# Two chained feed-forward stages: another order of their steps on ScalarE and TensorE, and an earlier first slot for all stages from the second one on

## The chip, the cores and the metric

The kernel runs on one core of a Trainium2 chip. Its time is device microseconds for one launch, taken as the median of the runs shown. Engine names are those of the profile: PE is TensorE's matmul side and PEld its weight loads, DVE is VectorE, ACT is ScalarE, POOL is GpSimd, SP is SyncE, which here only issues DMAs.

## What is computed

The input x has 128 sequences of 64 rows of 128 numbers. Four layers follow one another, and each adds two terms to x: a cross-attention of some kind and a feed-forward of some kind, each applied to the layer-normalised x and weighed by the tanh of a gate. The two feed-forwards that this change touches are those of layers 0 and 1. Both multiply with a 128x128 weight in 8-bit arithmetic:

```python
# layer 0 (lhs is layernorm(x))
lhs_scale = max(abs(lhs), over a row) / 127
acc = round(lhs / lhs_scale) @ round(rhs / rhs_scale)
x = x + gate * acc * lhs_scale * rhs_scale
# layer 1 (x is layernorm(x))
a_scale = max(abs(x), over a row)
y = round(x / a_scale * 127) @ w_quant.T
x = x + gate * y * (w_scale * a_scale / 127)
```

Between them stands layer 1's masked softmax attention (16 heads of 8), and behind them come layer 2's retention, layer 2's gated feed-forward, layer 3's softmax attention and, last and longest, layer 3's switch attention with routed experts.

## The kernel before, in words

x stays in SBUF as 64 tiles of 128 rows. After an opening (weights, context, layer 0's attention), the function `chain` runs six parts one behind the other and overlapping: `ff0` (feed-forward of layer 0), `at1` (softmax attention of layer 1), `ff1` (feed-forward of layer 1), `re` (retention), `gf` (gated feed-forward), `at3` (softmax attention of layer 3). Then `switch_attention` runs, which fills a little under two thirds of the span.

A part is a list of steps for each engine, each with a lag. Time is counted in slots. A part that begins at slot S and has pace 1 gives its item i to a step of lag L in slot S + i + L; with pace 2 it takes two items in a slot. `chained` writes out, for each engine, all steps of all parts in order of slot, within a slot in the order of the parts, and within a part in the order of the step list. So each engine's queue is a fixed order, and semaphores alone hold the engines together: a step that waits holds up everything behind it on its engine. The slots are no clock; an engine can be about a slot ahead of another.

`feed_forward_int` builds ff0 and ff1. Its item is a group of 4 tiles (16 groups). With the lag of each step in brackets, a group g goes through: DVE row statistics, aggregation and variance (1), POOL reciprocal root `rstd` (1), DVE negated mean (3), ACT `normalise` (3), DVE `absmax`, `scale`, `inverse` and, in layer 1, the output scale (4), ACT `shift` (5), which multiplies by 127 over the largest value and adds a large constant so that the sum is rounded, PE `turned` (5), four transposes into PSUM, ACT `keep` (6), which copies them to SBUF as bf16 and takes the constant off, PE `product` (6), DVE `output` (7), POOL `add` (7). In layer 0 POOL also spreads rows of layer 0's attention (`spread`, 0), PE turns them (0), DVE adds them to x (1), and POOL weighs the output before it adds it (7). In the order before, ACT's list is keep, normalise, shift, and PE's is product, turned.

`softmax_attention` (at1) has one tile per slot and begins at slot 12. Its lags run from 0 (row statistics) to 14 (the last addition to x, L1058), with normalise at 6 and the negated mean at 5, the projections at 8, the scores at 9, their reading, centring and exponential at 10, the turning of the probabilities at 11, the weighing of the values at 12. Tile 63 is therefore read last in slot 12 + 63 + 14 = 89. ff1's `turned` and `product` write PSUM banks in which at1 keeps its scores, and wait for at1's last score to be read (`after["turned"]`, slot 85). `re` waits for at1's last tile before it writes its SBUF buffers. In every slot that ff1 shares with at1, at1's steps stand ahead of ff1's on each engine; in a slot that ff0 shares with at1, ff0's stand ahead.

Of the kernel before, what the change touches and what calls it, by code (L numbers as in the profile page):

```python
# [54 lines left out]
def chained(parts, engine, eng):  # L55

    stages = [part.engines[engine](eng) if engine in part.engines else [] for part in parts]
    slots = [(part.start + t / part.pace, n, t) for n, part in enumerate(parts) if stages[n]
             for t in range(part.count + max(lag for lag, _ in stages[n]))]
    for _, n, t in sorted(slots):  # L60
        for lag, step in stages[n]:
            i = t - lag
            if 0 <= i < parts[n].count:
                step(i, i % parts[n].bufs, i // parts[n].bufs)


def once(step):

    def at(i, s, r):
        if i == 0:  # L70
            step()
    return at
# [685 lines left out]
def feed_forward_int(k, A, C, W, X, layer, OUT0, after):  # L758
# [113 lines left out]
    def scalar(act):  # L872
        def begin():
            act.preload_act_table(ACT.Exp)

        def normalise(g, s, r):
            act.wait_ge(q["nmr"], g + 1)
            for n in range(N):
                act.activation(xhat[:, s, n], tile(g, n), ACT.Identity, bias=small["nmr"][:, s, n:n + 1],
                               scale=small["rstd"][:, s, n:n + 1]).then_inc(q["xhat"], 1)  # L880

        def keep(g, s, r):
            act.wait_ge(q["turned"], g + 1)
            if g >= NB:
                act.wait_ge(q["product"], g - NB + 1)
            act.activation(qT[:, s], ps_q[g % 2], ACT.Copy, bias=-ROUND).then_inc(q["qT"], 1)

        def shift(g, s, r):
            act.wait_ge(q["inverse"], g + 1)
            if g >= NB:  # L890
                act.wait_ge(q["turned"], g - NB + 1)
            for n in range(N):
                act.activation(shifted[:, s, n], xhat[:, s, n], ACT.Copy, bias=ROUND,
                               scale=small["inv"][:, s, n:n + 1]).then_inc(q["shifted"], 1)
        return [(0, once(begin)), (6, keep), (3, normalise), (5, shift)]

    def tensor(pe):
        def turn_rows(g, s, r):
            pe.wait_ge(q["spread"], 2 * g + 2)
            if g >= 2:  # L900
                pe.wait_ge(q["added"], g - 1)
            for n in range(N):
                m = pe.transpose(ps_rows[g % 2][:, n], rows[:, g % 2, n], C["ident"][:])
            m.then_inc(q["rows"], 1)

        def turned(g, s, r):
            pe.wait_ge(q["shifted"], N * g + N)
            if g == 0 and layer == 1:
                pe.wait_ge(*after["turned"])
            if g >= 2:  # L910
                pe.wait_ge(q["qT"], g - 1)
            for n in range(N):
                m = pe.transpose(ps_q[g % 2][:, n], shifted[:, s, n], C["ident"][:])
            m.then_inc(q["turned"], 1)

        def product(g, s, r):
            pe.wait_ge(q["qT"], g + 1)
            if g == 0 and layer == 1:
                pe.wait_ge(*after["product"])
            if g >= 2:  # L920
                pe.wait_ge(q["y"], g - 1)
            for n in range(N):
                m = pe.matmul(ps_y[g % 2][:, n], qT[:, s, n], w16[:], start=True, stop=True)
            m.then_inc(q["product"], 1)
        return ([(0, turn_rows)] if layer == 0 else []) + [(6, product), (5, turned)]
    return Part(q, GROUPS, NB, gpsimd=gpsimd, vector=vector, scalar=scalar, tensor=tensor)


# [1428 lines left out]
def chain(k, A, C, W, X, CT, OUT0, x3):  # L2357

    nc = k.nc
    waits = {n: {} for n in ("at1", "ff1", "re", "gf", "at3")}
    with k.laid_over():
        at1 = softmax_attention(k, A, C, W, X, CT, 1, waits["at1"])
    with k.laid_over():
        at3 = softmax_attention(k, A, C, W, X, CT, 3, waits["at3"], x3)
    with k.laid_over(sbuf=False):
        re = retention(k, A, C, X, waits["re"])
    with k.laid_over():
        ff0 = feed_forward_int(k, A, C, W, X, 0, OUT0, {})  # L2370
    with k.laid_over():
        ff1 = feed_forward_int(k, A, C, W, X, 1, None, waits["ff1"])
    with k.laid_over(sbuf=False):
        gf = feed_forward_gated(k, A, C, W, X, waits["gf"])
    G, T = GROUPS, TILES
    waits["at1"].update(x=lambda i: (ff0.q["x"], i // GROUP + 1), a=(ff0.q["added"], G), qkv=(ff0.q["added"], G),
                        scores=(ff0.q["y"], G))
    waits["ff1"].update(buffers=(ff0.q["x"], G), x=at1.q["x"], turned=(at1.q["masked"], T), product=(at1.q["masked"], T))
    waits["re"].update(buffers=(at1.q["x"], T), x=ff1.q["x"], s1=(ff1.q["qT"], G), o=(ff1.q["y"], G))
    waits["gf"].update(buffers=(ff1.q["x"], G), x=re.q["x"], turn_x=(re.q["kT"], G), down=(re.q["x"], T),  # L2380
                       gate_up={0: [(re.q["wide"], HEADS // 2 * G), (re.q["probs"], T - 1)], 1: [(re.q["probs"], T)]},
                       turn_h={0: [(re.q["probs"], T)], 1: [(re.q["x"], T - 1)]})
    waits["at3"].update(buffers=(re.q["x"], T), x=lambda i: (gf.q["x"], i + 1), a=(gf.q["xT"], G),
                        qkv=(gf.q["hidden"], T), turned=(gf.q["hidden"], T), scores=(gf.q["hT"], T), o=(gf.q["x"], T))
    parts = [ff0.begins(0, 1), at1.begins(12, 1), ff1.begins(83, 1), re.begins(97, 2), gf.begins(131, 2), at3.begins(166, 2)]
    with nc.Block() as block:
        @block.sync
        def _(sp):
            chained(parts, "sync", sp)

        @block.gpsimd
        def _(pool):
            chained(parts, "gpsimd", pool)

        @block.vector
        def _(dve):
            chained(parts, "vector", dve)

        @block.scalar
        def _(act):  # L2400
            chained(parts, "scalar", act)

        @block.tensor
        def _(pe):
            chained(parts, "tensor", pe)
# [3 lines left out]
def program(nc, A, out):  # L2409
    k = Core(nc)  # L2410
    C, W = {}, {}
    scratch = {n: nc.dram_tensor("scratch_" + n, [S * 4 * S * 2], F32, kind="Internal") for n in ("lags", "circ")}
    x3 = nc.dram_tensor("scratch_x", [TILES * P * D], F32, kind="Internal").ap()\
        .rearrange("(t p d) -> t p d", p=P, d=D)
    with k.stack:
        constants(k, C)
        with k.scope():
            X = k.sb("x", [P, TILES, D])
            CT = k.sb("ctx_T", [P, TILES, P])
            prepared_weights(k, W)  # L2420
            OUT0 = k.sb("out0", [P, 2, TILES, 4])
            opening(k, A, C, W, X, CT, OUT0, scratch)
            with k.scope():
                chain(k, A, C, W, X, CT, OUT0, x3)
        switch_attention(k, A, C, x3, out)
# [23 lines left out]
```

## Time and profile before

| what | value |
|---|---|
| runs (median of 3) | 3125.66 us (3125.22, 3125.66, 3128.91) |
| the profiled execution's own time | 3124.05 us |
| its span, first to last instruction | 3122.3 us |
| granted TensorE clock over the span | 0.938 of full speed |
| PE, PEld busy | 92%, 70% |
| DVE, ACT, POOL busy | 87%, 75%, 70% |
| first step of ff0 / last addition of ff1 to x | 79.6 us / 546.5 us |

The profiled execution is 1.75 us longer than its span, and 1.6 us shorter than the median. The clock column of the profile is the share of full speed that was granted to TensorE; of its two levels 1.00 is 2.4 GHz and 0.50 is 1.2 GHz.

### The profile page before, as it was taken

To read this page: it belongs to the slowest core of one execution; us is meant where nothing else is said; L and a number is where in the kernel's file an instruction comes from. 1 tells how busy PE (TensorE), PEld (TensorE's weight loads), DVE (VectorE), ACT (ScalarE), POOL (GpSimd) and SP (SyncE) were. 2 spreads that over 40 slices of the span, in tenths; PEclk is the share of its full clock that TensorE was granted. 3 is DMA by queue.
4 is the path that set the end of the run, shared out by engine and by line. 5 is a ranking of instruction groups with operands and counts; after the bars stand their busy time and mean duration, and the time that the engine had idled before them with its cause. 6 is when DMAs were issued, how large, how long until landed. Compare 5 with 4: busy or idle time off the path is not lost.

```text
span 3122.3 us, 80587 instructions
## 1 busy us (share of the span) xinstructions
PE 2878.7 (92%) x25631; PEld 2189.3 (70%) x25644; DVE 2724.0 (87%) x9025; ACT 2348.9 (75%) x7674; POOL 2180.3 (70%) x3016
## 2 busy tenths in 40 slices
PE   7599984996689996999999999999999999999998
PEld 6367762674367774777777777777777777777776
DVE  6779977999979987988988889889889888898897
ACT  5667777779968875777777777777777777777776
POOL 2788866657944424777777777777777777777777
PEclk8589995997779997999999999999999999999999
DMA  5000001220000004000000000000000000000000
GB/s 132 8 2 3 3 2 31 76 68 1 1 8 18 18 20 130 7 9 7 9 8 7 9 8 7 9 8 7 9 7 9 8 7 9 8 7 9 8 6 6
DMA packets 114661, 55.46 MB, mean 18 GB/s; under 512 B 18496, under 2 KB 113856, under 8 KB 114240
## 3 DMA queue, kind: packets, MB, share of 16 engines
q1 hardware_dynamic: 114240, 50.30, 5.9%
q8 instruction: 209, 3.42, 0.5%
q14 instruction: 212, 1.74, 0.2%
HBM read 41.82 MB, written 8.45 MB: 16 GB/s over the span
## 4 chain that ended last, share of the span: by engine, by line
PE 60%; DVE 1%; ACT 1%; POOL 0%; issue 0%; DMA 0%; SPq 0%; POOLq 0%; ACTq 0%; DVEq 0%
PE ps_sw_a L2283 24%; PE ps_sw_d L2283 22%; PE ps_sw_w L2329 4%; PE ps_sw_w L2316 3%; PE ps_sw_s L2298 2%; PE ps_sw_s L2340 2%; PE ps_sw_m L2305 1%; ACT sw_scaled L2024 0%; DVE sw_v_part L2179 0%; PE ps_sw_m L2291 0%; DMA sw_v<-in_L_ffn_v_w 0%; ACT sw_probs L2073 0%; DVE sw_o_low L2125 0%; DVE sw_v_low L2118 0%; ACT sw_v_high L2079 0%
## 5 line engine op out<-in xcount | busy, mean ns | idle before, releaser
L2024 ACT ACTIVATE sw_scaled<-ps_sw_a,sw_gate_o 128x128 f32<-128x128 f32 x2048 | 620.4, 447 | 253.9 <-PE ps_sw_a L2283 246.7
L2024 ACT ACTIVATE sw_scaled<-ps_sw_a,sw_gate_v 128x128 f32<-128x128 f32 x2048 | 597.7, 449 | 193.8 <-PE ps_sw_a L2283 192.1
L2179 DVE SCALAR_TENSOR_TENSOR sw_o_part<-ps_sw_d,sw_gate_o,sw_o_part 128x128 f32<-128x128 f32 x1920 | 555.4, 339 | 62.8 <-PE ps_sw_d L2283 60.2
L1951 POOL TENSOR_TENSOR sw_v_pair<-sw_v_part,sw_scaled 128x256 f32<-128x256 f32 x512 | 382.1, 746 | 154.6 <-DVE sw_v_part L2179 88.5
L2179 DVE SCALAR_TENSOR_TENSOR sw_v_part<-ps_sw_d,sw_gate_v,sw_scaled 128x128 f32<-128x128 f32 x1024 | 304.2, 338 | 123.5 <-PE ps_sw_d L2283 106.4
L1977 POOL TENSOR_TENSOR sw_o_rest<-sw_o_rest,sw_scaled 128x256 f32<-128x256 f32 x384 | 285.3, 743 | 157.7 <-ACT sw_scaled L2024 120.5
L2179 DVE SCALAR_TENSOR_TENSOR sw_v_part<-ps_sw_d,sw_gate_v,sw_v_part 128x128 f32<-128x128 f32 x1024 | 305.1, 339 | 0.0
L1980 POOL TENSOR_TENSOR sw_o_rest<-sw_o_rest,sw_scaled 128x256 f32<-128x256 f32 x384 | 282.9, 737 | 30.1
L1956 POOL TENSOR_TENSOR sw_v<-sw_v_pair 128x128 f32<-128x128 f32 x512 | 244.2, 477 | 40.1
L2283 PE MATMUL ps_sw_a<-sw_v_high,sw_xT_high 128*128 128x512 f32 x512 | 234.1, 457 | 8.2 <-DVE sw_v_low L2118 8.2
L2283 PE MATMUL ps_sw_a<-sw_o_high,sw_ctx_high 128*128 128x512 f32 x512 | 215.5, 421 | 0.2 <-ACT sw_scaled L2024 0.2
L1030 POOL TENSOR_TENSOR at_key_wide<-at_keyT,c_quarter_heads 128x512 f32<-128x512 f32 x128 | 133.1, 1040 | 109.5 <-ACT at_keyT L1168 109.5
L2283 PE MATMUL ps_sw_d<-sw_v_high,sw_xT_high 128*128 128x512 f32 x512 | 207.5, 405 | 0.4 <-DVE sw_v_part L2179 0.4
L2283 PE MATMUL ps_sw_d<-sw_o_high,sw_ctx_high 128*128 128x512 f32 x512 | 202.1, 395 | 1.2 <-DVE sw_v_part L2179 1.2
L2283 PE MATMUL ps_sw_d<-sw_o_low,sw_ctx_high 128*128 128x512 f32 x512 | 202.8, 396 | 0.0
L2283 PE MATMUL ps_sw_a<-sw_o_high,sw_ctx_low 128*128 128x512 f32 x512 | 202.7, 396 | 0.0
L2283 PE MATMUL ps_sw_a<-sw_v_high,sw_xT_low 128*128 128x512 f32 x512 | 202.0, 395 | 0.0
L2283 PE MATMUL ps_sw_d<-sw_o_high,sw_ctx_low 128*128 128x512 f32 x512 | 202.0, 395 | 0.0
L2283 PE MATMUL ps_sw_a<-sw_o_low,sw_ctx_high 128*128 128x512 f32 x512 | 201.9, 394 | 0.0
L2283 PE MATMUL ps_sw_d<-sw_v_high,sw_xT_low 128*128 128x512 f32 x512 | 201.5, 394 | 0.0
L2283 PE MATMUL ps_sw_a<-sw_v_low,sw_xT_high 128*128 128x512 f32 x512 | 201.5, 394 | 0.0
L2283 PE MATMUL ps_sw_d<-sw_v_low,sw_xT_high 128*128 128x512 f32 x512 | 200.2, 391 | 0.0
(337 smaller groups left out, 8467.2 us busy)
## 6 DMA issues: line engine op xcount, KB each, us to landing
re_values<-in_ctx SPq DMA_DIRECT2D x128, 64.0 KB, 2.3
l_ctx<-in_ctx SPq DMA_DIRECT2D x16, 256.0 KB, 5.4
x<-in_x SPq DMA_DIRECT2D x16, 256.0 KB, 5.4
re_ctx<-in_ctx SPq DMA_DIRECT2D x16, 256.0 KB, 3.1
scratch_x<-x SPq DMA_DIRECT2D x64, 64.0 KB, 1.5
sw_x<-scratch_x SPq DMA_DIRECT2D x64, 64.0 KB, 1.9
sw_x_res<-scratch_x SPq DMA_DIRECT2D x64, 64.0 KB, 1.8
out<-sw_y SPq DMA_DIRECT2D x64, 64.0 KB, 1.5
```

The costliest lines, as they stand in the source:

```text
L1030: pool.tensor_tensor(key_wide[:, s], keyT[:, s].unsqueeze(1).broadcast_to([P, QUARTER, P]), C["quarter_heads"][:].unsqueeze(2).broadcast_t ...
L1951: pool.tensor_tensor(v_pair[:, h % 2], v_part[:, h], scaled[:, h % 4, 2:4], ALU.add)\
L1956: pool.tensor_tensor(v[:, h], v_pair[:, h % 2, 0], v_pair[:, h % 2, 1], ALU.add).then_inc(q["v"], 1)
L1977: pool.tensor_tensor(o_rest[:, 0:2], o_rest[:, 0:2], scaled[:, h % 4, 0:2], ALU.add)\
L1980: pool.tensor_tensor(o_rest[:, 2:4], o_rest[:, 2:4], scaled[:, h % 4, 2:4], ALU.add)\
L2024: act.activation(scaled[:, h % 4, e], ps_a[h % 2][:, e], ACT.Copy, scale=gates[:, s, h, HALF_E + e:HALF_E + e + 1]).then_inc(a_scaled[kind ...
L2179: dve.scalar_tensor_tensor(out=acc[:, e % 2], in0=ps_d[h % 2][:, e], scalar=gates[:, s, h, e:e + 1], in1=before, op0=ALU.mult, op1=ALU.add ...
L2283: m = pe.matmul(bank, lhs[a], w[b][:, h, experts], start=c == 0, stop=c == 2)
L2298: m = pe.matmul(ps_s[t, h], probs[t, s, h], C["ident"][t, t], start=True, stop=True)
L2316: m = pe.matmul(ps_w[n][:, h * P:(h + 1) * P], W["pair"][:, 4 * n + h], xT[:, s], start=True, stop=True)
L2329: m = pe.matmul(ps_w[b][:, h * S:(h + 1) * S], v[t, h], probs_T[t, h], start=True, stop=True)
L2340: m = pe.matmul(ps_s[t], xT[:, s, t], uT[:, :, t], start=True, stop=True)
```

## The change

The step lists of `feed_forward_int` are reordered on two engines, for both feed-forwards, and four start slots in `chain` are lowered by three. No instruction is added or removed, none changes its shape, and no wait is changed.

```diff
-        return [(0, once(begin)), (6, keep), (3, normalise), (5, shift)]
+        return [(0, once(begin)), (3, normalise), (5, shift), (6, keep)]
...
-        return ([(0, turn_rows)] if layer == 0 else []) + [(6, product), (5, turned)]
+        return ([(0, turn_rows)] if layer == 0 else []) + [(5, turned), (6, product)]
...
-    parts = [ff0.begins(0, 1), at1.begins(12, 1), ff1.begins(83, 1), re.begins(97, 2), gf.begins(131, 2), at3.begins(166, 2)]
+    parts = [ff0.begins(0, 1), at1.begins(12, 1), ff1.begins(80, 1), re.begins(94, 2), gf.begins(128, 2), at3.begins(163, 2)]
```

The first line is ACT's list, the second PE's. ff1's groups now go through slots 81 to 102 in place of 84 to 105, retention and what follows keep their distance to ff1.

## Rows read from the trace of the kernel before

**Rows 1.** The page: span, and the granted clock in 40 slices
```profile
span 3122.3 us, 80587 instructions
...
PEclk8589995997779997999999999999999999999999
```

**Rows 2.** Windows: us, busy time of each engine (instructions), granted clock, DMA share, GB/s
```profile
96.00:141.00 45.00, 26.32 (x120) 19.26 (x120) 36.13 (x168) 32.95 (x91) 38.94 (x47) 0.50 0.00 1
...
190.00:440.00 250.00, 245.02 (x4090) 188.78 (x4090) 227.26 (x552) 196.99 (x453) 203.51 (x183) 1.00 0.01 3
433.45:454.00 20.55, 17.07 (x287) 12.70 (x283) 16.95 (x45) 13.83 (x27) 14.79 (x12) 0.99 0.01 2
454.00:472.03 18.03, 9.58 (x88) 7.91 (x88) 10.64 (x63) 11.62 (x31) 4.28 (x5) 0.50 0.10 30
472.03:503.16 31.13, 12.05 (x56) 7.41 (x56) 20.09 (x107) 22.74 (x63) 16.08 (x15) 0.50 0.06 18
```

**Rows 3.** Timeline of ACT in ff1: start, us, engine, line, operation [idle before <-releaser]
```profile
495.70 0.60 ACT L886 ACTIVATE ff_qT<-ps_ff_q 128x512 bf16<-128x512 f32 x1 [1.20 <-PE ps_ff_q L913]
496.19 1.63 ACT L879 ACTIVATE ff_xhat<-x,ff_nmr,ff_rstd 128x128 f32<-128x128 f32 x4
497.73 1.27 ACT L893 ACTIVATE ff_shifted<-ff_xhat,ff_inv 128x128 f32<-128x128 f32 x4
500.20 0.60 ACT L886 ACTIVATE ff_qT<-ps_ff_q 128x512 bf16<-128x512 f32 x1 [1.20 <-PE ps_ff_q L913]
```

**Rows 4.** Timeline of PE in that slot of ff1
```profile
499.05 1.11 PE L913 MATMUL ps_ff_q<-c_ident,ff_shifted 128*128 128x128 f32 x4 [2.09 <-ACT ff_shifted L893]
```

**Rows 5.** Timeline of DVE, the same slot of ff1
```profile
497.86 0.69 DVE L817 TENSOR_REDUCE ff_amax<-ff_xhat 128x4 f32<-128x512 f32 x1 [1.62 <-ACT ff_xhat L879]
...
500.50 0.17 DVE L866 TENSOR_SCALAR ff_var<-ff_mv 128x4 f32<-128x4 f32 x1
500.58 0.16 DVE L811 SCALAR_TENSOR_TENSOR ff_nmr<-ff_mv,ff_rstd 128x4 f32<-128x4 f32 x1
```

**Rows 6.** Timeline of POOL in ff0, one slot
```profile
118.26 0.73 POOL L801 COPY ff_rows<-out 128x256 f32<-128x256 f32 x2
119.22 1.02 POOL L786 TENSOR_TENSOR ff_rstd<-ff_var,minus_half 128x4 f32<-128x4 f32 x1 [0.22 <-DVE ff_var L866]
120.21 1.27 POOL L792 TENSOR_TENSOR ff_y<-ff_y,w_ff_scale 128x512 f32<-128x512 f32 x1
121.55 1.27 POOL L795 TENSOR_TENSOR x<-x,ff_y 128x512 f32<-128x512 f32 x1
```

**Rows 7.** Timeline where at1 begins beside ff0
```profile
152.88 0.48 ACT L1135 ACTIVATE at_xhat<-x,at_nmr,at_rstd 128x128 f32<-128x128 f32 x1
...
157.35 0.28 ACT L1174 ACTIVATE at_xT<-ps_at_a 128x128 f32<-128x128 f32 x1 [1.03 <-PE ps_at_a L1263]
```

**Rows 8.** Timeline of DVE and POOL: short DVE steps beside POOL's
```profile
510.46 1.02 POOL L786 TENSOR_TENSOR ff_rstd<-ff_var,minus_half 128x4 f32<-128x4 f32 x1 [2.97 <-DVE ff_var L866]
...
510.68 0.13 DVE L811 SCALAR_TENSOR_TENSOR ff_nmr<-ff_mv,ff_rstd 128x4 f32<-128x4 f32 x1
...
511.45 1.27 POOL L795 TENSOR_TENSOR x<-x,ff_y 128x512 f32<-128x512 f32 x1
512.08 0.67 DVE L828 TENSOR_SCALAR ff_scale<-ff_amax 128x4 f32<-128x4 f32 x1
...
550.77 1.71 DVE L1394 SCALAR_TENSOR_TENSOR re_nmr<-re_mv,re_rstd 128x4 f32<-128x4 f32 x1
550.84 1.62 POOL L1359 TENSOR_TENSOR re_k_part<-re_ctx,re_rot 128x256 f32<-128x256 f32 x2
```

**Rows 9.** Timeline of DVE where at1 ends beside ff1
```profile
433.45 0.28 DVE L1058 TENSOR_TENSOR x<-ps_at_a,x 128x128 f32<-128x128 f32 x1
...
472.03 0.86 DVE L839 BATCH_NORM_STATS2 ff_stats<-x 128x6 f32<-128x128 f32 x4
```

**Rows 10.** Source view of L1058: count, ns min/median/max, first and last start us
```profile
L1058 DVE TENSOR_TENSOR x<-ps_at_a,x x64: 280/281/292, 190.4 to 468.8; 128x128 f32<-128x128 f32 x64
```

## The prediction

> **What bounds the kernel now.** The page comes first: it gives the span, and its clock row shows two dips in the first 900 us, at the second to fourth slice and at the sixth and seventh [rows 1]. The windows over these stretches tell what goes on there. Between 190 and 440 us, where at1 runs alone, PE is busy 98% at full clock. Beside ff0 (96 to 141) and in ff1 (472 to 503) TensorE has half the clock and PE is busy 58% and 39% of the time, and no other engine is full either: in ff1 ACT has 22.7 us of 31.1, DVE 20.1, POOL 16.1 [rows 2]. Where nothing is full, a loop of waits sets the pace, and the timeline of one slot shows which.
>
> On ACT the keep starts at 495.70 behind 1.20 us of idle time that ended with PE's transposes; then normalise, then shift; the next keep starts at 500.20, again behind 1.20 us [rows 3]. PE's transposes start at 499.05, when the shift is done, and take 1.11 [rows 4]. So the slot of 4.50 us is keep 0.49, normalise 1.54, shift 1.27, transposes with their semaphores 1.20. The transposes of a group run behind its shift, and ACT has nothing to do in between, since keep stands at the head of its list. DVE waits 1.62 us for the normalised group in each slot: of 4.50 it works 2.88 [rows 5].
>
> **The reorder in ff1.** With keep at the end of the slot the transposes it needs were made in the slot before, during ACT's own work. What remains on ACT is 0.49 + 1.54 + about 1.2 = 3.25 us a slot. I check the others against that: DVE 2.88 of work [rows 5], POOL 1.02 for the root and 1.27 for the addition = 2.3 [rows 8], PE 1.11 and a product shorter than that. The product now waits for a keep that comes last, and DVE's output takes it in the next slot, some 4.0 us after the slot's normalise began; output, aggregation, variance and negated mean behind it need 1.2 more, and the normalise that they release is due at 6.5. So that loop has 1.3 us in hand. ACT sets 3.25.
>
> The slots that hold ff1 alone are 90 to 96 before: from the seventh group's statistics at 472.03 to 503.16, 31.1 us for 7 [rows 2, 9]. Three of them go away by the earlier start, and the other four take 4 x 3.25 = 13.0. Lower bound of the slot 2.9 (DVE's work), upper 4.5 (as before).
>
> **The earlier start.** It takes no work away: three slots' worth of ff1 moves from slots of its own into slots 81 to 83 of at1, and each later group meets more of at1 than it did. Before, slots 81 to 89 last from 433.45 to 472.03, 38.6 us [rows 9]. An at1 slot takes 4.4 us (the first to the 64th addition is 278.4 us for 63 slots [rows 10]), with DVE busy 91%, 4.0 us a slot, of which some 0.6 has run out by slot 81 (the row statistics of at1), so 3.4. To this come 1.4 of ff1's row steps in slots 81 to 83 and 2.3 in 84 and 85 (DVE's 2.88 less the output), while at1's own part falls to about 2.9. That is 4.8, 4.8, 4.9, 5.2, 5.3, DVE-bound, sum 25.0. In 86 to 89 the clock is at half, as before [rows 2], PE has at1's last turns and weighings together with ff1's transposes, and at1's steps of each slot start behind a product that waits for the late keep; I take 6.0, 4.7, 4.5, 3.8, sum 19.0 (from 454 to 472, about the same four slots, it was 18.0 [rows 2]). Waits that such a sum does not hold, and ff1's table load, which moves to slot 80 where ACT has less spare time: 2.7. Together 46.7, 8.1 more than before. Bounds: 41.6, if the added steps go into idle time as far as there is any, and 58, if each shared slot runs the chains of both parts one after the other.
>
> ff1 and at1's end: 38.6 + 31.1 before, 46.7 + 13.0 after, gain 10.0.
>
> **Beside retention.** In its slots 94 to 96 ff1 still has all its steps and retention adds mostly DVE work (memsets, statistics), so DVE binds at about 4.0 where the loop had 4.5: 1.5 us. From then on DVE was the bound before already, and I add 0.5 for the keeps that waited. Gain 2.0, bounds 0 and 4. All parts behind keep their distance to each other and their periods: nothing. SP's fetches for retention wait for at1's last tile and still have five slots of ff1 in front of their first reader.
>
> **The reorder in ff0.** The same loop gives 4.50 there, but POOL is nearly full: 38.9 of 45.0 [rows 2]. One slot goes from 118.26 to the next spread at 122.77, with 0.22 idle; spread, root, weighing and addition make 4.3 [rows 6]. So the nine slots 7 to 15 gain 0.2 each, 1.8. Slot 6, before POOL's additions start, gains 0.7. In slot 16 spread is over, but at1's first root joins root, weighing and addition: 4.5 again, no gain, and DVE stands until that root is there, since at1's first negated mean is in its list before ff0's next steps. In slots 17 and 18 POOL has only 2.3 to 3.5, and ACT's 3.25 against 4.50 counts: 1.2 each. So at1's first normalise (slot 18, behind ff0's three steps on ACT), now at 152.88 [rows 7], comes 0.7 + 1.8 + 2.4 = 4.9 us earlier. In slots 19 to 22 ff0 runs out; the keep no longer waits there either, but PE now has the product behind the transposes, and at1's first matmuls behind both. I take these as cancelling, less 0.3: 4.6. The bounds are 1.8 (only POOL's slots gain) and 7.5 (the 1.2 counts in slots 6 and 17 to 20, five times, beside the 1.8).
>
> **Sum.** 10.0 + 2.0 + 4.6 = 16.6. The profiled execution took 3124.05, so 3107.45, and the median of the runs is 1.6 above it: 3109.
>
> **The locks between DVE and POOL** could undo part of it. DVE's scale of 128x4 numbers, 0.17 us alone, took 0.67 when it was issued at 512.08 beside POOL's addition, and ended with it at 512.75; the negated mean at 510.68 took 0.13 beside POOL's root, so the root does not hold it [rows 8]. In the new slot of ff1 POOL has root and addition back to back behind DVE's variance, busy until 2.4 us after it. The scale is issued about 0.8 us after the variance, in the root, and is not held; if ACT makes DVE wait it falls into the addition and is held for up to 1.27, which the slot that DVE is ahead absorbs. So I count nothing. At 550.77, though, a short step took 1.71 us, across both of two POOL steps that followed each other [rows 8]; if that happened here, the scale would wait 1.6 us, and DVE's slot would be 2.88 + 1.6 = 4.5, no better than before. The Trainium skill (SBUF — State Buffer, "Who interferes with whom") says that the port pair the two engines share is an exclusive lock, held for a whole instruction, so that the second to issue blocks fully. The addition's row agrees (0.67 for 0.17), the root's row does not (0.13). By that rule alone the root would hold the scale too, 0.35 us a slot: 3.23, still within ACT's 3.25, unless the lock passes straight to the addition, which is the rival below.
>
> **Rivals.**
> Locks set ff1's slot (4.45 in place of 3.25) and keep ff0's nine slots at 4.50: 4 x 1.2 + 1.8 = 6.6 less, 3116. For it speaks the row of 1.71, against it that of 0.67 with POOL's next step free to start. Chance 0.12.
> The clock falls earlier. PE's share in slots 81 to 85 goes down as these get longer, and the clock went to half in this stretch already, at about 454 [rows 2]. At half, at1's 4.3 us of matmuls a slot (98% of 4.4) take up to twice as long, some 7 against my 4.8 to 5.3; for four slots about 8 us: 3117. Chance 0.15.
> The shared slots take nearly nothing, since DVE and ACT both had idle time: the lower bound 41.6 gives 5 more, and ff0's upper bound 3 more: 3101. Chance 0.12.
> Slower: both junctions go serial. PE's list puts the product, which waits for the last copy of a slot, ahead of all of at1's steps of the next, and these feed ACT. If the shared slots of ff1 reach the upper bound of 58, ff1's side becomes 58 + 13 = 71 against 69.7, and the same coupling takes ff0's 4.6 and some more: 3127 to 3132. It decides from about 57 us for slots 81 to 89, 6.3 a slot. Against it: the last four of them took 4.5 each before [rows 2]. Chance 0.03.
> Nothing changes, since the start was not what held ff1 and the order binds elsewhere: 3126, 0.03; the 1.20 of idle time in each slot speaks against it.
>
> **Numbers.** Forecast 0.55, by its own range 3104 to 3114. The range 3101 to 3119 takes in the locks, the clock and the cheap overlap. What a measurement of this kernel can tell from no change is about 0.2%, 6.3 us: faster than 3119.4 I give 0.9, within 0.2% 0.06, slower 0.04.
>
> **What would show it.** ff1's keep in slots 90 to 93 every 3.2 to 3.3 us with no idle time before it, the normalise not waiting; absmax's wait of 1.62 gone; ff0's keeps every 4.3 us with POOL without gaps; at1's last addition to x later behind its first by some 8 us than now. Wrong: ff_scale with a mean well over 0.17, a keep period over 4 in ff1, the clock at 0.5 before at1's scores are through, or at1's first normalise less than 3 us earlier.

## The result, and the profile of the changed kernel

The median over the runs is 3122.36 us (3117.05 to 3133.31, 22 runs) against 3128.83 us of the kernel before (3125.22 to 3135.24, 22 runs on the same chip). The ratio is 0.9980 with a 95% interval of 0.9972 to 0.9987: 6 us faster by ratio and medians, where 16.6 was forecast. (The forecast of 3109 was made from a median before of 3125.66; that median is 3128.83 here, so 3.2 us of the 13 between forecast and time are not the change's.) The profiled execution took 3119.42 us around a span of 3117.6, 4.7 us less than the span of before [rows 1].

The page of the changed kernel, its first line and its clock row. The two dips of the clock are still there.

```profile
span 3117.6 us, 80600 instructions
...
PEclk8589985997789997999999999999999999999999
```

Windows of the changed kernel. The columns are those of [rows 2]. Slot 81 begins at 429.91, at the 56th addition to x of at1 (433.45 before), slot 90 at 486.62, with ff1's statistics there (472.03 before), and slot 94, retention's first, at 499.14. Slot 94 of this kernel stands against slot 97 of the kernel before, at 503.16.

```profile
96.00:141.00 45.00, 26.02 (x128) 21.62 (x128) 42.35 (x179) 34.94 (x97) 40.02 (x48) 0.50 0.00 1
429.91:450.00 20.09, 14.89 (x248) 10.95 (x244) 19.71 (x64) 13.97 (x31) 14.22 (x12) 1.00 0.00 1
450.00:486.62 36.62, 16.37 (x144) 14.00 (x141) 19.86 (x90) 20.77 (x56) 10.12 (x9) 0.50 0.07 19
486.62:499.10 12.48, 5.89 (x33) 4.58 (x32) 11.43 (x61) 12.48 (x37) 8.99 (x9) 0.50 0.11 33
```

This table is the finding: **slots 81 to 89 took 56.7 us in place of 38.6**, the slots of ff1 alone 12.5 (four) in place of 31.1 (seven). Of the 18.6 us won behind slot 90, 18.1 were paid ahead of it. DVE is full until 450 (19.71 of 20.09, where a slot takes 5.6 against 4.5 before); from 450 to 486.62 no engine is: ACT has 20.77 of 36.62, DVE 19.86, PE 16.37. That is again the picture of a loop of waits, the one that the reorder took out of ff1's own slots, now in the slots that ff1 shares with at1.

In ff1's own slots ACT works without a break. Its timeline there answers to [rows 3]: the keep no longer waits, and the period is 3.18 us, against 4.50.

```profile
489.07 0.57 ACT L886 ACTIVATE ff_qT<-ps_ff_q 128x512 bf16<-128x512 f32 x1
489.55 1.64 ACT L879 ACTIVATE ff_xhat<-x,ff_nmr,ff_rstd 128x128 f32<-128x128 f32 x4
491.08 1.27 ACT L893 ACTIVATE ff_shifted<-ff_xhat,ff_inv 128x128 f32<-128x128 f32 x4
492.25 0.58 ACT L886 ACTIVATE ff_qT<-ps_ff_q 128x512 bf16<-128x512 f32 x1
```

DVE in the same slot, against [rows 5]: the reduction follows the negated mean at once, and the 1.62 us of waiting ahead of it are gone.

```profile
488.70 0.16 DVE L811 SCALAR_TENSOR_TENSOR ff_nmr<-ff_mv,ff_rstd 128x4 f32<-128x4 f32 x1
488.78 0.68 DVE L817 TENSOR_REDUCE ff_amax<-ff_xhat 128x4 f32<-128x512 f32 x1
```

Now the shared slots, first one row of slot 81 and POOL's beside it. DVE's variance step, 0.17 us elsewhere, takes 0.88 and ends at 433.03, with POOL's step at 433.01:

```profile
431.97 1.04 POOL L1030 TENSOR_TENSOR at_key_wide<-at_keyT,c_quarter_heads 128x512 f32<-128x512 f32 x1
...
432.15 0.88 DVE L866 TENSOR_SCALAR ff_var<-ff_mv 128x4 f32<-128x4 f32 x1
```

Then slot 85 and parts of 86, all engines, rows picked out in order of time. Read what stands in brackets first: it is the idle time of the engine ahead of the row, and what ended it.

```profile
452.35 0.28 DVE L1058 TENSOR_TENSOR x<-ps_at_a,x 128x128 f32<-128x128 f32 x1
...
452.51 1.90 POOL L1023 TENSOR_TENSOR at_probs<-at_raw,at_top 128x1024 f32<-128x1024 f32 x1 [1.41 <-DVE at_top L1086]
...
452.83 0.29 DVE L1066 TENSOR_TENSOR at_heads_out<-ps_at_o,at_rsum 128x128 f32<-128x128 f32 x1
453.04 1.39 DVE L811 SCALAR_TENSOR_TENSOR ff_nmr<-ff_mv,ff_rstd 128x4 f32<-128x4 f32 x1
...
454.45 1.06 ACT L1159 ACTIVATE at_probs<-at_probs 128x1024 f32<-128x1024 f32 x1 [1.44 <-POOL at_probs L1023]
...
455.41 1.63 ACT L879 ACTIVATE ff_xhat<-x,ff_nmr,ff_rstd 128x128 f32<-128x128 f32 x4
...
456.95 1.26 ACT L893 ACTIVATE ff_shifted<-ff_xhat,ff_inv 128x128 f32<-128x128 f32 x4
...
458.27 1.12 PE L913 MATMUL ps_ff_q<-c_ident,ff_shifted 128*128 128x128 f32 x4 [5.89 <-ACT ff_shifted L893]
...
459.18 0.42 PE L1194 MATMUL ps_at_a<-c_ident,at_heads_out 128*128 128x128 f32 x1
...
460.11 0.28 ACT L1144 ACTIVATE at_heads_T<-ps_at_a 128x128 f32<-128x128 f32 x1 [1.90 <-PE ps_at_a L1194]
460.48 0.29 DVE L1058 TENSOR_TENSOR x<-ps_at_a,x 128x128 f32<-128x128 f32 x1 [3.92 <-ACT at_heads_T L1144]
...
466.99 0.58 ACT L886 ACTIVATE ff_qT<-ps_ff_q 128x512 bf16<-128x512 f32 x1
...
468.05 0.63 PE L923 MATMUL ps_ff_y<-w_ff,ff_qT 128*128 128x128 bf16 x4
...
469.78 0.29 DVE L1058 TENSOR_TENSOR x<-ps_at_a,x 128x128 f32<-128x128 f32 x1 [4.25 <-ACT at_heads_T L1144]
```

Slot 85 lasts from 452.35 to 460.48, 8.1 us (an at1 slot alone takes 4.4). The chain through it: at1's centre on POOL (1.9), the exponential on ACT behind it, then ff1's normalise and shift, which stand behind the exponential in ACT's list. PE stands still for 5.89 us for that shift, since ff1's transposes (L913) are next in its list. Behind them in the same list is at1's turn of the heads of slot 86 (L1194), whose input DVE had made by 453.12 (L1066). It runs at 459.18, ACT copies its result at 460.11, and DVE, after 3.92 us of idle time, adds to x at 460.48. In slot 86 the product (L923), behind the keep of 466.99, comes ahead of the next turn of the heads in the same way, and DVE idles 4.25 us. Two of the rows show a second, smaller loss: DVE's negated mean, 0.15 us elsewhere, takes 1.39 at 453.04 and ends with POOL's centre. The same step took 1.07 in slot 83 and 1.40 in slot 84. In slots 81 to 84, where DVE is full, the time by which its short steps are held comes to 3.0 us (0.71 and 0.14 for the variance in 81 and 82, 0.92 and 1.25 for the negated mean in 83 and 84).

In ff0, POOL's timeline of one slot, to be held against [rows 6]: root, next spread and next root follow without idle time, and from root to root it takes 4.39 us.

```profile
113.84 1.02 POOL L786 TENSOR_TENSOR ff_rstd<-ff_var,minus_half 128x4 f32<-128x4 f32 x1
...
117.38 0.74 POOL L801 COPY ff_rows<-out 128x256 f32<-128x256 f32 x2
118.23 1.02 POOL L786 TENSOR_TENSOR ff_rstd<-ff_var,minus_half 128x4 f32<-128x4 f32 x1
```

The first normalise of at1, which stood at 152.88 [rows 7]:

```profile
149.19 0.48 ACT L1135 ACTIVATE at_xhat<-x,at_nmr,at_rstd 128x128 f32<-128x128 f32 x1
```

Counted from ff0's first statistics (82.31 before, 82.44 here) that is 66.75 us against 70.57, 3.8 less.

### The profile page after: what moved, and what is told of

Same layout as the page of the kernel before. It is cut to its first block, busy times and chain, and to the rows that moved or that the text cites. A ratio compares the mean times of both kernels' runs of the same rounds, so it can differ in the third digit from the quotient of the medians.

```text
span 3117.6 us, 80600 instructions
## 1 busy us (share of the span) xinstructions
PE 2875.1 (92%) x25644; PEld 2192.7 (70%) x25644; DVE 2735.1 (88%) x9025; ACT 2352.2 (75%) x7674; POOL 2185.0 (70%) x3016
## 4 chain that ended last, share of the span: by engine, by line
PE 60%; ACT 1%; DVE 1%; POOL 0%; issue 0%; DMA 0%; SPq 0%; POOLq 0%; ACTq 0%
PE ps_sw_a L2283 24%; PE ps_sw_d L2283 22%; PE ps_sw_w L2329 4%; PE ps_sw_w L2316 3%; PE ps_sw_s L2298 2%; PE ps_sw_s L2340 2%; PE ps_sw_m L2305 1%; ACT sw_scaled L2024 0%; PE ps_sw_m L2291 0%; DVE sw_v_part L2179 0%; DVE sw_v_low L2118 0%; ACT sw_probs L2073 0%; DMA sw_v<-in_L_ffn_v_w 0%; ACT sw_v_high L2079 0%; PE ps_sw_w L2346 0%
## 5 line engine op out<-in xcount | busy, mean ns | idle before, releaser
L2073 ACT ACTIVATE sw_probs<-ps_sw_s,sw_shift 128x64 f32<-128x64 f32 x512 | 197.4, 479 | 4.6 <-DVE sw_shift L2240 4.6
```

What stands on the lines that cost most here:

```text
L2073: act.activation(probs[:, s, h], ps_s[:, h], ACT.Exp, bias=shift[:, s, h:h + 1], scale=float(P) ** -0.5, accum_out=total[:, s, h:h + 1]).t ...
```

## The experiments

The table gives all runs at a glance, and the text behind it takes them by the question that each answers. "Shared" is from the start of slot 81 to that of slot 90, "alone" from there to retention's first slot, read from the profiled run as above. The sum of the two is the time from slot 81 to retention. Ratios are to runs of the kernel before on the same chip. The first column has the names by which the runs are called below. The expectations weigh two theories: that the fixed lists of the engines make these slots long, called Q and later 1 (the steps of at1 stand in them behind steps of ff1 that wait), and that something else does, called D (DVE's work and its waits for POOL) and later 2 (the same and the half clock).

| kernel | list order | ff1 begins | shared us | alone us (slots) | sum | ratio (95% interval) |
|---|---|---|---|---|---|---|
| before | old | 83 | 38.6 | 31.1 (7) | 69.7 | 1 |
| the change | new | 80 | 56.7 | 12.5 (4) | 69.2 | 0.9980 (0.9972 to 0.9987) |
| order_only | new | 83 | 37.2 | 22.7 (7) | 59.9 | 0.9946 (0.9931 to 0.9961) |
| start_only | old | 80 | 56.0 | 17.1 (4) | 73.1 | 1.0016 (1.0002 to 1.0030) |
| order_start85 | new | 85 | 33.1 | 27.6 (9) | 60.7 | 0.9957 (0.9940 to 0.9974) |
| turned_later | new, see below | 80 | 50.5 | 14.7 (4) | 65.2 | 0.9979 (0.9970 to 0.9988) |
| lists_apart | new, see below | 80 | 47.7 | 14.7 (4) | 62.4 | 0.9969 (0.9957 to 0.9980) |
| filled | new | 80 | 58.5 | 12.8 (4) | 71.3 | 1.0004 (0.9992 to 1.0015) |
| order_start82 | new | 82 | 43.7 | 18.9 (6) | 62.6 | 0.9965 (0.9953 to 0.9977) |
| order_start84 | new | 84 | 34.0 | 25.4 (8) | 59.4 | 0.9948 (0.9935 to 0.9960) |
| mean_early | new | 80 | 52.9 | 12.1 (4) | 65.0 | 0.9975 (0.9963 to 0.9988) |
| apart_mean_early | new, see below | 80 | 45.6 | 14.7 (4) | 60.3 | 0.9969 (0.9959 to 0.9979) |
| ff1_order | new in ff1 alone | 83 | 39.3 | 22.7 (7) | 62.0 | 0.9966 (0.9952 to 0.9979) |
| scalar_only | new on ACT alone | 83 | 39.9 | 22.2 (7) | 62.1 | 0.9960 (0.9947 to 0.9972) |

**The two halves apart.** order_only takes the new lists and leaves the starts; start_only the reverse.

```diff
-    parts = [ff0.begins(0, 1), at1.begins(12, 1), ff1.begins(80, 1), re.begins(94, 2), ...
+    parts = [ff0.begins(0, 1), at1.begins(12, 1), ff1.begins(83, 1), re.begins(97, 2), ...
```

> The new order on ScalarE and TensorE with the old start slots (83, 97, 131, 166). Theory Q (TensorE's list): in the changed kernel the slots that ff1 shares with at1 are long because the transposes of ff1 stand in TensorE's list ahead of at1's steps of the next slot and wait for a shift that comes behind at1's exponential on ScalarE; with the old start only slots 88 and 89 hold such transposes, so slots 81 to 89 take 39 to 41 us (56.7 in the changed kernel), the seven slots of ff1 alone 3.2 each, 22.3, and ff0 keeps its 4: the time is 10 to 13 us below before, so 4 to 6 below the changed kernel. Theory D (VectorE is the bound of the shared slots, through its work and its waits for GpSimd's steps): an earlier start is worth what it was forecast to be less a few us; order alone gives no more than the changed kernel does, 5 to 7 us.

> The old order with the new start slots (80, 94, 128, 163). Theory Q: the shared slots take 56 us or more, the four slots of ff1 alone 4.5 each, 18, together 74 or more against 69.7 before, and nothing is gained in ff0: slower than before by 3 to 9 us. Theory D: the start moves 3 slots of 4.5 under at1 for some 8 to 10 us of added work: faster by 3 to 5 us.

The order alone gains 0.54% by the ratio, 17 us, and 14 by the medians (3126.87 and 3112.95). With the start as well the gain is 0.20%, 6 us. So **the earlier start costs 8 to 11 us in the new order**, and alone, in the old one, it costs 0.16%, 5 us. The windows of order_only: shared 37.21, alone 22.67, ACT busy in all of the latter.

```profile
435.73:472.94 37.21, 24.75 (x369) 19.04 (x365) 27.58 (x109) 24.82 (x57) 19.09 (x16) 0.81 0.05 16
472.94:495.61 22.67, 11.15 (x58) 8.86 (x59) 20.08 (x107) 22.67 (x65) 14.52 (x14) 0.50 0.08 24
```

In start_only ACT's keep still waits the 1.20 us for PE in each slot alone, as in [rows 3], and the shared slots are as long as with the change:

```profile
501.21 0.60 ACT L886 ACTIVATE ff_qT<-ps_ff_q 128x512 bf16<-128x512 f32 x1 [1.20 <-PE ps_ff_q L913]
```

```profile
440.14:496.15 56.01, 34.51 (x388) 26.65 (x385) 39.77 (x153) 34.67 (x85) 24.32 (x21) 0.64 0.05 14
```

The 56 us are thus a matter of the start, with either order of the lists. Both runs went theory Q's way: order_only gained 14 to 17 us where it had said 10 to 13, start_only lost 3 to 5 where it had said 3 to 9.

**A ladder of starts.** The new order with 85, 84 and 82, by the same one-line edit.

> The new order with ff1 two slots later than before (85, 99, 133, 168), so that the first transposes of ff1 come in slot 90, behind at1's last step. Theory Q: slots 81 to 89 lose the coupling, 36 to 38 us, and nine slots of ff1 alone at 3.2 give 28.6; together 65 to 67, 3 to 5 less than before, and with ff0's 4 the time is 7 to 9 us below before, about that of the changed kernel or 1 to 3 below it, although it has five more slots of ff1 alone. Theory D: each slot later costs 3.2 and saves at most 2 of VectorE's work, so this is 5 us or more slower than the changed kernel.

> The new order with ff1 at slot 84. Start 83 measured ratio 0.9946, start 85 0.9957, start 80 0.998. Theory 1: the shared slots take about 34 us and 8 slots of ff1 alone 25.5 to 26, ratio 0.994 to 0.9955, no worse than start 83, since one slot less of ff1's transposes lies in at1's tail. Theory 2: 35.5 + 26, 1 to 2 us slower than start 83, ratio 0.995 to 0.9955.

> The new order with ff1 at slot 82 (the other starts one slot earlier than before as well). With start 83 the shared slots 81 to 89 took 37.2 us and 7 slots of ff1 alone 22.7; with 80 56.7 and 12.5. Theory 1 (each slot in which ff1's transposes stand ahead of at1's tail costs 6 to 6.5 us more than one without them, and saves 3.2): 43.5 + 19.5, 3 us more than with start 83, ratio to before about 0.9955. Theory 2 (work of VectorE: an earlier slot adds 1.4 to 2.9 us of it and saves 3.2): 39.5 + 19.5, the same time as with start 83 or 1 us less, ratio 0.994 to 0.9945.

The sum of shared and alone is 60.7, 59.4, 59.9, 62.6, 69.2 for 85, 84, 83, 82, 80. Each slot that is moved saves about 3.2 of the slots alone. What it costs in the shared ones goes 0.9, 3.2, 6.5 and then 13.0 for two: nearly free while at1 runs out, 6.5 once ff1's transposes stand in the list from slot 87 on. For 82 theory 1 had 43.5 and 19.5, and 43.7 and 18.9 came; theory 2's 39.5 is ruled out. The transposes are not all of that 6.5, though: slot 87 is 3.1 longer than with 83, but slot 85, which holds none of them, is 1.9 longer. There the clock had already fallen and DVE idles 1.99 us for a copy of at1 that stands behind ff1's normalise on ACT. For 85 the sum expected was 65 to 67, and 60.7 came, 13 us below before by the ratio where 7 to 9 were expected: a still later start costs less than thought. The ratios put 83 and 84 level (0.9946 and 0.9948). The kernel before had its start where the new order also wants it.

**Taking the wait out of PE's list.** turned_later runs ff1's transposes, keep and product one slot later; lists_apart goes on until nobody waits for a step of the same slot's end: transposes one slot behind the shift, product one slot behind the keep. Both leave ff0 as in the change. Of lists_apart:

```diff
-        return ... + [(5, turned), (6, product)]                                    # PE
+        return ... + [(6, turned), (7, product)]
-        steps += [(4, scale), (1, moments), (4, inverse), (7, output), (1, aggregate)]   # DVE
+        steps = [(3, negated_mean), (8, output), (4, absmax)] + ...
-        return ... + [(1, rstd), (7, add)]                                          # POOL
+        return ... + [(1, rstd), (8, add)]
```

(ACT's list stays as it is, keep at lag 6. turned_later has the same lags but for the keep, which stands at 7, in the slot of the product.)

> The changed kernel (start 80) with ff1's transposes, keep and product one slot later on their engines (lags 6, 7, 7), its output and addition at lag 8, the output ahead of absmax in VectorE's list; ff0 as changed. The transposes of a group then stand behind at1's steps of the slot after the shift and do not wait. ff1 takes one slot more alone, 3.2. Theory Q: slots 81 to 89 fall from 56.7 to 44 to 48, ff1's side is 60 to 64 against 69.7 before: 9 to 13 us below before. Theory D: the shared slots stay above 53 and the slot more costs 3.2: 1 to 3 us above the changed kernel.

> The changed kernel (start at slot 80), with ff1's lists uncoupled altogether: its transposes stand one slot behind its shift, its keep in the slot of the transposes, its product one slot behind the keep, its output and addition one slot later. PE and DVE then wait in no slot for a copy that ScalarE makes at the end of the same slot. Theory 1 (TensorE's list: at1's steps wait behind ff1's transposes and product): the shared slots 81 to 89, 56.7 us in the changed kernel and 50.6 with the transposes alone moved, fall to 45 to 48; time 3114 to 3117 us, ratio to before about 0.996. Theory 2 (VectorE's work, its short steps held by GpSimd, and the half clock set these slots): they stay at 50 or above, ratio about 0.998, as the changed kernel. The four slots of ff1 alone stay at 3.1 to 3.7 us each by either.

turned_later took 6 us off the shared slots, to 50.5 where theory Q had said 44 to 48, and nothing off the whole: its ratio is that of the change (0.9979 and 0.9980), where 9 to 13 us below before were expected. What was left on PE is the product: it still waited for the keep of its own slot, with at1's turn of the heads behind it.

```profile
472.01 0.61 PE L924 MATMUL ps_ff_y<-w_ff,ff_qT 128*128 128x128 bf16 x4 [3.77 <-ACT ff_qT L886]
...
472.40 0.42 PE L1196 MATMUL ps_at_a<-c_ident,at_heads_out 128*128 128x128 f32 x1
```

lists_apart takes this off too, and the shared slots fall to 47.7, **9.0 us less than with the change**. Its rows of slot 85, where the same normalise and shift follow the same centre and exponential as above:

```profile
457.94 1.63 ACT L879 ACTIVATE ff_xhat<-x,ff_nmr,ff_rstd 128x128 f32<-128x128 f32 x4
...
459.48 1.26 ACT L893 ACTIVATE ff_shifted<-ff_xhat,ff_inv 128x128 f32<-128x128 f32 x4
460.65 0.25 ACT L1146 ACTIVATE at_heads_T<-ps_at_a 128x128 f32<-128x128 f32 x1
...
461.00 0.29 DVE L1060 TENSOR_TENSOR x<-ps_at_a,x 128x128 f32<-128x128 f32 x1 [1.91 <-ACT at_heads_T L1146]
...
462.41 1.06 PE L914 MATMUL ps_ff_q<-c_ident,ff_shifted 128*128 128x128 f32 x4
```

PE has no idle time ahead of ff1's transposes here (ahead of those of slot 87, at 470.43, it still has 2.02 us). But DVE still waits 1.91 us, for a copy on ACT (L1146) that stands behind ff1's shift. ACT's list couples the two parts as well, and this part is not removed in any run. The later output is paid for: in the slots alone ACT now waits for DVE, and a slot takes 3.68 in place of 3.13.

```profile
488.99 1.26 ACT L879 ACTIVATE ff_xhat<-x,ff_nmr,ff_rstd 128x128 f32<-128x128 f32 x3 [0.38 <-DVE ff_nmr L811]
```

Beside retention it is paid for too: from retention's first slot to its first addition to x it takes 52.4 us in lists_apart, 52.6 in turned_later and 51.6 in apart_mean_early (below), against 50.0 with the change. So of the 9.0 us in the shared slots 2.2 go in the slots alone and 2.4 here, and 4.4 are left; the ratio, 0.9969 for 0.9980, says 3.4. The 3114 to 3117 us that theory 1 expected were not reached (3120.1). The edit also takes one group's transposes, product and output (1.1 us of PE, 0.6 of PE, 0.7 of DVE) out of the shared slots; in slots 85 to 88 they get 11.2 us shorter, and slot 89 gets 2.2 longer.

**Is it the clock?** In slots 85 to 89 TensorE has half the clock (0.50 from 450 on). filled keeps the change as it is and gives PE more to do: 8 transposes of the identity ahead of at1's turns of its last five tiles, 8 ahead of ff1's first five transposes, 4 ahead of its first four products, none of them read by anyone.

```diff
+                if masked and part == 0 and i >= 59:
+                    for n in range(8):
+                        pe.transpose(ps_t[:, n % 4], C["ident"][:], C["ident"][:])
                 pe.wait_ge(q["exp"], i + 1)
...
+            if layer == 1 and g < 5:
+                for n in range(8):
+                    pe.transpose(ps_q[g % 2][:, n % 4], C["ident"][:], C["ident"][:])
             pe.wait_ge(q["shifted"], N * g + N)
```

> The changed kernel, with idle time of TensorE filled by transposes of the identity whose results nobody reads: 8 ahead of at1's turns of the last five tiles (before the wait for the exponential), 8 ahead of ff1's first five transposes and 4 ahead of its first four products (before the waits for the shift and the keep). If the granted clock stays up between 450 and 485 us: by theory 2 (half clock) the shared slots fall from 56.7 to 47 or less and the time to about 3113 us; by theory 1 (the order of the lists) only the PE steps on the chain get shorter, 13.8 us of busy PE at half clock in these 31 us, of which perhaps half lies on it: shared slots 53, time about 3119 us, ratio 0.997. If the clock falls all the same, the added 1.3 to 2.6 us a slot are hidden or cost up to 5 us, and it tells nothing of the clock.

Windows of filled, slots 84, 85 and 86:

```profile
450.30:456.80 6.50, 5.14 (x77) 4.08 (x76) 6.40 (x21) 4.31 (x9) 2.91 (x2) 1.00 0.00 0
456.80:464.90 8.10, 2.57 (x15) 2.34 (x14) 4.11 (x19) 4.16 (x11) 2.91 (x2) 0.69 0.01 2
464.90:474.00 9.10, 6.59 (x86) 5.95 (x85) 2.98 (x17) 4.65 (x12) 1.01 (x1) 0.90 0.00 0
```

The clock was 1.00, 0.69 and 0.90 there, where the changed kernel had it at half from 450 on, and the slots took 6.5, 8.1 and 9.1 us against 6.5, 8.1 and 9.3. In slot 85 the three rows that matter stand as far apart as above: PE's transposes 5.75 us behind the start of the centre (5.76 with the change), the addition 7.95 behind it (7.97).

```profile
456.94 1.90 POOL L1029 TENSOR_TENSOR at_probs<-at_raw,at_top 128x1024 f32<-128x1024 f32 x1 [1.41 <-DVE at_top L1092]
...
462.69 1.11 PE L916 MATMUL ps_ff_q<-c_ident,ff_shifted 128*128 128x128 f32 x4 [5.53 <-ACT ff_shifted L893]
...
464.89 0.29 DVE L1064 TENSOR_TENSOR x<-ps_at_a,x 128x128 f32<-128x128 f32 x1 [3.92 <-ACT at_heads_T L1150]
```

So slots 84 and 85 do not hang on the clock: what fills them lies on POOL and ACT. For slot 86 the run says less, since 1.92 us of the added transposes lie in its own chain (at 464.23): that it took 9.1 all the same, against 9.3, leaves room for up to about 2 us that the clock gave back, by an estimate from these numbers. Slot 87 took 7.7 at a clock of 0.69, against 7.6 at half. Neither theory's number came (47 or less, and 53): the shared slots took 58.5. The whole kernel was 7 us slower than the change by the ratios, of which 2.1 lie in ff1's slots; where the rest comes from is not shown.

Slot 86 of other runs does show a price of the clock, in the absence of ff1's transposes. It took 6.21 us before the change, and 4.84 in order_only, with the same number of instructions on PE. In order_only the clock fell within the slot (0.66 over it). In the kernel before and in scalar_only, whose slot 86 takes 6.21 too, it fell ahead of the slot (0.50). PE, busy throughout, took 1.90 us for at1's weighing at half clock and 1.11 at full:

```profile
457.45 1.11 PE L1206 MATMUL ps_at_o<-at_val_wide,at_probs_T 128*64 128x18 f32 x32
```

```profile
453.36 1.90 PE L1206 MATMUL ps_at_o<-at_val_wide,at_probs_T 128*64 128x18 f32 x32
```

The first row is order_only's, the second scalar_only's. So the whole difference between the 37.2 us of order_only's shared slots and the 38.6 before comes by way of the clock.

**The negated mean and POOL.** In mean_early ff1's negated mean moves to the end of DVE's slot before; apart_mean_early joins this and lists_apart.

```diff
-        steps = [(3, negated_mean), (4, absmax)] + ...
+        steps = [(4, absmax)] + ...
...
+        steps += [(2, negated_mean)]        # last in the slot, ff1 only
```

> The changed kernel (start 80), with ff1's negated mean moved to the end of VectorE's slot before, where GpSimd computes a root and not at1's centre: in the changed kernel it stood in the centre's time and took 1.40 and 1.39 us at 446.50 and 453.04 in place of 0.15. Theory 1 (the lists of TensorE and ScalarE set slots 85 to 88, VectorE only 81 to 84): slot 84 gets 1.2 us shorter, slot 85 does not, because there its normalise stands behind the exponential anyway; shared slots 55.5 of 56.7, ratio unchanged within 0.1%. Theory 2 (the lock on VectorE is a main cause): 54 or less, and the slots behind follow.

> Both: ff1's lists uncoupled as in the kernel with 47.7 us of shared slots and ratio 0.9969, and the negated mean early. If the lock costs its 1.2 us in two or three slots beside what the lists cost: shared slots 44.5 to 45.5, ratio about 0.996. If it is hidden there: 47 to 48 and the same ratio.

One line of the groups over the shared slots, of the changed kernel and of mean_early (busy us, mean ns):

```profile
L811 DVE SCALAR_TENSOR_TENSOR ff_nmr<-ff_mv,ff_rstd 128x4 f32<-128x4 f32 x8 | 4.6, 578 | 0.0
```

```profile
L811 DVE SCALAR_TENSOR_TENSOR ff_nmr<-ff_mv,ff_rstd 128x4 f32<-128x4 f32 x8 | 1.3, 157 | 0.0
```

3.3 us of DVE time are gone, and the shared slots are 3.8 shorter, 52.9: theory 1's 55.5 is missed, and the condition of theory 2 (54 or less) is met. But the slots show that most of it is not the hold. Slots 83 and 84, where the negated mean had been held, are 1.0 shorter in all (5.68 to 5.45, 6.54 to 5.78); slots 85 and 86 are as long as they were (8.1, 9.3). Slots 87 and 88 give 2.3 and 0.6, and there the negated mean had taken 0.15 in the changed kernel too: it stood in DVE's list behind at1's reciprocal, which waits for PE, and ACT waited 2.20 us for it (at 471.89). That is the lists again, DVE's this time. Joined to lists_apart it brings 2.1 more, 47.7 to 45.6: 1.0 in slots 83 and 84, 1.1 in slot 87. That is close to the 44.5 to 45.5 expected for a hold of 1.2 us in two or three slots, but half of it came by the other way, and the ratio stays at 0.9969.

The hold itself was in part handed on. In mean_early the variance of slot 83 takes 0.89 (at 445.98; 0.17 with the change), and beside POOL's centre of 449.40 the reduction runs at its own length, and the scale behind it takes 0.69 in place of 0.17:

```profile
449.40 1.90 POOL L1024 TENSOR_TENSOR at_probs<-at_raw,at_top 128x1024 f32<-128x1024 f32 x1 [1.44 <-DVE at_top L1087]
...
449.93 0.68 DVE L817 TENSOR_REDUCE ff_amax<-ff_xhat 128x4 f32<-128x512 f32 x1
...
450.64 0.69 DVE L828 TENSOR_SCALAR ff_scale<-ff_amax 128x4 f32<-128x4 f32 x1
```

**Which list, which feed-forward.** ff1_order has the new order in ff1 alone, scalar_only the new order on ACT alone, both with start 83.

```diff
-        return ... + [(5, turned), (6, product)]
+        return ... + [(6, product), (5, turned)]        # scalar_only; ff1_order: so, and ACT's old list, in ff0 alone
```

> The new order in ff1 alone, ff0 in the old one, start 83. Against both in the new order (ratio 0.9946) it lacks what ff0 gains, 3.8 us by the profiles (70.6 us from ff0's first statistics to at1's first normalise before, 66.7 in the new order), so ratio about 0.9958; ff1's own slots take 3.2 us and the shared ones 37 us. If ff0's gain is taken back in at1's filling, whose time varies from profile to profile by more than that, the ratio is 0.9946 again.

> ScalarE's new order alone, TensorE in its old one (product ahead of the transposes), start 83. If ScalarE's list is what held the loop: the same 3.2 us a slot in ff1 and ratio 0.9946 as with both orders, since the product and the transposes together (1.7 us) fit into the 2.8 us of normalise and shift. If TensorE's order matters, the transposes come late behind the product and the slot is 3.5 us or more, ratio above 0.9955.

In scalar_only ACT's keeps are 3.19 us apart, without idle time: ScalarE's list is what held ff1's loop, and the order of PE's two steps does nothing for it.

```profile
479.16 0.58 ACT L886 ACTIVATE ff_qT<-ps_ff_q 128x512 bf16<-128x512 f32 x1
...
482.35 0.58 ACT L886 ACTIVATE ff_qT<-ps_ff_q 128x512 bf16<-128x512 f32 x1
```

The ratios, 0.9966 and 0.9960, are above the 0.9946 of order_only, with overlapping intervals. For ff1_order 0.9958 was expected, which lies in its interval; for scalar_only 0.9946, which lies just outside (0.9947 to 0.9972). In both profiles the shared slots took 2 to 3 us more than in order_only. Slot 86 accounts for 1.4 of that: it took 6.2 us in them, as before, and 4.8 in order_only, with the clock at 0.50 in place of 0.66 (above). That PE's order is worth nothing to the whole is therefore not shown, only that ff1's own slots do without it.

## Why the prediction was right and wrong, point by point

**The slot of ff1 alone: right.** 3.25 was forecast for four slots, 13.0 in all; 12.5 came, 3.13 a slot, with ACT at work all the time, and the wait ahead of the reduction gone.

**The slots shared with at1: wrong, and this is the step that failed.** The prediction had 46.7 for slots 81 to 89, 8.1 more than before; it was 56.7, 18.1 more. Its parts: 25.0 for slots 81 to 85 against 30.6, and 19.0 for 86 to 89 against 26.1. What failed is the 2.7 us that the sum set aside for waits: 12.7 came. In slots 81 to 84 the sum had 19.7 and 22.4 came, 2.7 more. DVE was full there, as the sum had it, and its short steps were held by POOL's for 3.0 us; without that time the sum of DVE's work fits to 0.3 us. In slots 85 to 89 it had 24.3 and 34.3 came, 10.0 more, and there no engine is full: the fixed lists are what the sum left out. lists_apart shows this, with 9.0 us less in the shared slots once ff1's transposes and product stand one slot behind what they wait for; 4.4 of these outlive the later output. With the negated mean moved as well the same start gave 45.6, 1.1 us from the forecast, but that closeness is partly luck: slots 81 to 85 took 27.6 against 25.0, 86 to 89 18.0 against 19.0, and one group's last steps had been moved out of them. How the 10.0 us divide between PE's, ACT's and DVE's lists and the half clock is shown in part only. I had argued for the 4.5 us a slot of the last four shared slots from the kernel before. But there ff1's transposes stood in slots 88 and 89, where at1 had little more than its last outputs left; with the earlier start they stand from slot 85 on, beside at1's last scores, turns and weighings, and no row of before shows that meeting.

**The rival that came nearest** was the slower one, with a chance of 0.03. Its mechanism is what happened on ff1's side: the product and the transposes ahead of at1's steps in PE's list. It put the break-even at about 57 us for these slots, and 56.7 came, just short of it: ff1's side took 69.2 us against 69.7, so it gained half a microsecond where 10.0 was forecast. Its loss in ff0 did not come about, and so its 3127 to 3132 us did not either.

**The locks** were counted at nothing. I looked for them at the scale in ff1's own slots, and there they cost nothing (0.17 for each). In the shared slots two other short steps, the variance and the negated mean, met longer steps of POOL, of at1. They held DVE for 3.0 us where it was the bound; moving the negated mean gave 1.0 of them back.

**The clock as a rival** had its condition met, since it was down from 450 on, but in slots 84 and 85, which are 1.3 and 2.8 us longer than forecast, it made no difference. In slots 86 to 89 its share stays open.

**ff0: right in kind.** 4.6 was forecast, by at1's first normalise 4.9, and 3.8 was seen there. The one of POOL's nine slots shown above takes 4.39, where 4.3 was computed; at1's first addition came 4.1 earlier (186.31 against 190.40). That this gain reaches the end is not shown: in order_only the first normalise was as early, counted from ff0's first statistics (66.7 us), and yet slot 81 began at 435.73, later than before (433.45).

**Beside retention: smaller.** From retention's first slot to its first addition it took 50.0 us in place of 50.6: 0.6, where 2.0 was taken within bounds of 0 and 4.

**The sum.** In the profiles slot 81 comes 3.5 us earlier, ff1's side adds 0.5, the start of retention 0.6: 4.6. The end is 4.7 earlier. Behind these the stages of retention, gf, at3 and the switch attention differ by -0.7, -0.8, +3.6 and -2.0, and I do not put this down to the change: at3's stage, +3.6, took 285.8 us before and 285.7 in lists_apart, 282.2 with the change and in order_only, 280.1 in start_only and order_start85, without regard to the edits. So the agreement of 4.6 with 4.7 rests in part on these cancelling.

## What to carry to other kernels

Where each engine runs a fixed list, do not price an overlap by work alone. For each slot in which two parts will share the lists, ask of every wait what stands behind it on its engine, and whose next step that is, and ask of every short step of DVE which step of POOL it will now stand beside; do it for the slots to which the step will move, not for those in which it is seen now. A start and an order are two changes: here the order was worth 14 to 17 us and the start, made on top of it, gave 8 to 11 of them back, which the run of each alone shows at once.

## What the runs showed of the hardware

**Which short steps of DVE are held by POOL.** Beside the centre (1.90 us, 128x1024) the negated mean took 1.39 and 1.40 us and the scale 0.69 (in mean_early), and each ended with the centre; beside the 128x512 step of 1.04 us the variance took 0.88 in place of 0.17, and ended with it; the reduction of 128x512 (0.68) and the steps that read PSUM, such as the heads' output (0.29), ran at their own length. The negated mean reads two tiles in SBUF. The Trainium skill (SBUF — State Buffer, "Who interferes with whom") says this of such steps: two inputs in SBUF contend with a GpSimd instruction that reads it, a tensor_scalar can, a reduction never does. The rows agree here (scale and variance are such tensor_scalars), and [rows 8] still do not: the same negated mean took 0.13 beside POOL's root.

**The same kernel part at different lengths.** at1's filling, from its first normalise to its first addition, took 37.5 us before, 37.1 with the change, 36.0 in order_start85 and 42.7 in start_only, where the clock from 160 to 190 us was 0.50 (0.66 before, 0.71 with the change). Single profiles of this kernel therefore tell nothing under some 5 us about a whole span. The ratios of the medians do, and so do slots whose rows are alike from run to run: slots 83 to 85 took 5.68, 6.54 and 8.13 us with the change and 5.68, 6.53 and 8.12 in start_only.
